# Order of the slots on PE in a macaron layer (MoE, attention, MoE): gate, up and down in one run, attention visits two by two

## The reference, cut to what matters

```
x = x + 0.5 * ffn(layernorm(x))
x = x + attention(layernorm(x))
x = x + 0.5 * ffn(layernorm(x))
```

```
g, u = split(x @ w_gu.T)
acc += (silu(g) * u) @ w_d.T * combine[:, expert]
```

## Time and profile before

| what | value |
|---|---|
| median of 3 runs | 2342.43 us (2339.06 to 2343.24) |
| profiled execution, its own time | 2340.71 us |
| its span, first to last instruction | 2338.9 us |
| mean granted TensorE clock over the span | 0.998 |
| PE busy | 2241.6 us, 96% |
| DVE busy | 1580.5 us, 68% |
| ACT busy | 1236.9 us, 53% |
| POOL busy | 1051.4 us, 45% |
| matmuls L1071 (gate, up) | 9216 |
| matmuls L1089 (down) | 4608 |
| matmuls L1134 (values) | 2048 |
| matmuls L1101 and L1113 (scores) | 1024 each |

### The profile page before, as it was taken

One profiled execution on the slowest core, in us unless ns is written; L12 is line 12 of the kernel. 1 busy time (PEld: TensorE's weight loads), 2 busy tenths in 40 slices (PEclk: granted clock), 3 DMA queues, 4 the chain that ended last, 5 costly groups with the idle time before them and its releaser, 6 DMA issues.

```text
span 2338.9 us, 47968 instructions
## 1 busy us (share of the span) xinstructions
PE 2241.6 (96%) x19280; PEld 1499.3 (64%) x19280; DVE 1580.5 (68%) x3131; ACT 1236.9 (53%) x1966; POOL 1051.4 (45%) x863
## 2 busy tenths in 40 slices
PE   0899999999999999999999999999999999999999
PEld 0788875555565566555555565655655665688887
DVE  7657578877777877777877876776776753355543
ACT  3333331566566666566566566656656666533332
POOL 0667663433443443443434433433433434466665
PEclk9999999999999999999999999999999999999999
DMA  5211121001101011101101111010010010001010
GB/s 198 78 38 33 30 57 37 20 16 40 25 21 42 21 25 32 41 3 40 45 6 45 24 31 32 11 41 11 22 35 16 12 39 10 20 28 30 19 38 19
DMA packets 111446, 77.78 MB, mean 33 GB/s; under 512 B 57460, under 2 KB 103796, under 8 KB 110840
## 3 DMA queue, kind: packets, MB, share of 16 engines
q1 hardware_dynamic: 111080, 74.69, 11.6%
q10 hardware_dynamic: 144, 0.03, 0.0%
HBM read 62.87 MB, written 11.80 MB: 32 GB/s over the span
## 4 chain that ended last, share of the span: by engine, by line
PE 89%; DVE 8%; issue 2%; ACT 0%; DMA 0%; POOL 0%; POOLq 0%; DVEq 0%; ACTq 0%
PE PS L1071 42%; PE PS L1089 21%; PE PS L1101 11%; PE PS L1134 10%; DVE arena L871 1%; PE PS L1113 1%; PE PS L1030 1%; PE PS L1053 1%; PE PS L1175 1%; PE PS L1161 1%; DVE turned L839 1%; DVE turned L837 1%; DVE arena L843 1%; DVE arena L848 1%; DVE arena L836 0%
## 5 line engine op out<-in xcount | busy, mean ns | idle before, releaser
L1071 PE MATMUL PS<-XT,WGU 128*128 128x256 f16 x9216 | 1117.6, 274 | 64.4 <-DVE WGU L725 31.4
L1071 PEld LDWEIGHTS PS<-XT,WGU 128*128 128x128 f16 x9216 | 876.8, 98 | 290.7 <-issue 141.8
L535 POOL TENSOR_TENSOR arena<-arena 128x512 f16<-128x512 f32 x384 | 447.9, 1166 | 1163.6 <-ACT arena L610 1163.6
L871 DVE TENSOR_REDUCE arena<-PS 128x1 f32<-128x512 f32 x1024 | 658.1, 685 | 354.5 <-PE PS L1101 352.7
L633 ACT ACTIVATE arena<-PS,fac 128x512 f32<-128x512 f32 x1024 | 646.4, 684 | 249.2 <-PE PS L1113 247.8
L603 ACT ACTIVATE arena<-PS,fac 128x512 f32<-128x512 f32 x384 | 263.9, 687 | 718.8 <-PE PS L1071 718.8
L1089 PE MATMUL PS<-WD,arena 128*128 128x256 f16 x4608 | 568.0, 273 | 3.2 <-POOL arena L535 1.6
L1089 PEld LDWEIGHTS PS<-WD,arena 128*128 128x128 f16 x4608 | 431.9, 98 | 144.8 <-issue 90.6
L530 POOL TENSOR_TENSOR arena<-arena 128x512 f32<-128x512 f32 x384 | 491.9, 1281 | 47.2 <-DVE arena L856 45.2
L848 DVE SCALAR_TENSOR_TENSOR arena<-arena,PS 128x512 f32<-128x512 f32 x384 | 261.2, 680 | 278.6 <-ACT arena L603 278.1
L1101 PE MATMUL PS<-arena 48*128 48x512 f16 x1024 | 311.7, 381 | 2.7 <-DVE arena L871 2.2
(11 more groups left out here) (112 smaller groups left out, 788.4 us busy)
## 6 DMA issues: line engine op xcount, KB each, us to landing
arena<-ce_scratch SPq DMA_DIRECT2D x256, 128.0 KB, 3.3
arena<-wgu SPq DMA_DIRECT2D x2, 3072.0 KB, 15.0
arena<-q_scratch SPq DMA_DIRECT2D x192, 32.0 KB
arena<-ktab_c SPq DMA_DIRECT2D x16, 256.0 KB, 4.1
q_scratch<-arena SPq DMA_DIRECT2D x32, 128.0 KB, 1.7
out<-X SPq DMA_DIRECT2D x8, 512.0 KB, 2.9
X<-wd SPq DMA_DIRECT2D x1, 3072.0 KB, 25.3
X<-x SPq DMA_DIRECT2D x1, 3072.0 KB, 14.6
```

The lines of the kernel that those rows point to most:

```text
L535: pool.tensor_tensor(hs[1][:, d % HS, :], tw[d % 2], hs[0][:, d % HS, :], ALU.subtract).then_inc(lo_done, 1)
L871: dve.tensor_reduce(mx[:, half * REP * QT + c:half * REP * QT + c + 1], PS[:, B_MAX + half, :], AX_X, ALU.max).then_inc(max_taken, 1)
L1071: ins = pe.matmul(PS[:, b, j * HALF_G:(j + 1) * HALF_G], WGU[w][:, kt, part * CHUNKS + c + j, :], XT[r][:, k % 2, kt, half * HALF_G:(half ...
```

## The change

The table of visits gives positions 2 and 3 in every slot and positions 0 and 1 in addition in every tenth slot (slots d with (d - 64) % 10 == 9); while v is below 0, all four. PE's iteration becomes: gate of d+1, positions 0 and 1 (every tenth slot), up of d+1, down of d-1, positions 2 and 3, one event. An even visit comes first and an odd one second, so a block is scores, values, scores. The event table holds one event for each slot: fixed events keep their slots, and out_T, tok_T and out_y go to the next slot that is free. The loops of ACT and DVE get the same places. By the two tables, visit 0 moves from slot 77 to 74 and the last visit from 310 to 307.

```diff
--- before.py
+++ after.py
@@ -72,6 +72,7 @@
 QKV = 3
 RING = 3
 HEAD_AT = (1, 3, 0, 2)
+EXTRA_EVERY = 10
 FIRST = 2 * PER_GROUP + 16
 
 
@@ -79,7 +80,7 @@
 
     at, v, d = {}, -AHEAD, FIRST
     while v < VISITS + 2:
-        for pos in range(3 if v < 0 or (d - FIRST) % 5 == 4 else 2):
+        for pos in range(0 if v < 0 or (d - FIRST) % EXTRA_EVERY == EXTRA_EVERY - 1 else 2, 4):
             if v < VISITS + 2:
                 at[d, pos] = v
                 v += 1
@@ -128,21 +129,17 @@
                 at[k * PER_GROUP + s].append((name, k + 1, 0))
 
     def place(d, event):
-        while len(at[d]) > 1:
+        while at[d]:
             d += 1
         at[d].append(event)
         return d
 
-    done = 0
-    for hv in range(2 * UNITS):
-        d = place(max(done, SLOT_OF[quad_visit(8 * hv + 7)] + 1), ("out_T", hv, 0))
-        done = d
-        if hv % 4 == 3:
-            d = place(d + 3, ("tok_T", hv // 4, 0))
-            d = place(d + 1, ("tok_T", hv // 4, 1))
-            d += 1
-            for j in range(4):
-                d = place(d + 1, ("out_y", hv // 4, j))
+    turned_at = [place(SLOT_OF[quad_visit(8 * hv + 7)] + 1, ("out_T", hv, 0)) for hv in range(2 * UNITS)]
+    for v in range(2 * UNITS // 4):
+        d = place(turned_at[4 * v + 3] + 3, ("tok_T", v, 0))
+        d = place(d + 1, ("tok_T", v, 1)) + 1
+        for j in range(4):
+            d = place(d + 1, ("out_y", v, j))
     return at
 
 
@@ -669,8 +666,9 @@
                 k, s = divmod(d, PER_GROUP)
                 if d + 1 < SLOTS:
                     gate(d + 1)
-                if (d, 0) in VISIT:
-                    visit(VISIT[d, 0])
+                for pos in range(2):
+                    if (d, pos) in VISIT:
+                        visit(VISIT[d, pos])
                 if 0 <= d < SLOTS:
                     high(d)
                 if 1 <= k <= GROUPS:
@@ -683,12 +681,9 @@
                         rows_high(norm_of_group(k + 1))
                     if s == T_LOGITS + 1:
                         exponentials(k + 1)
-                if (d, 1) in VISIT:
-                    visit(VISIT[d, 1])
-                if len(EVENTS[d]) > 1:
-                    event(d, 1)
-                if (d, 2) in VISIT:
-                    visit(VISIT[d, 2])
+                for pos in range(2, 4):
+                    if (d, pos) in VISIT:
+                        visit(VISIT[d, pos])
                 if EVENTS[d]:
                     event(d, 0)
 
```

## The result

The changed kernel takes 2472.94 us (median of 4 runs, 2467.82 to 2475.31), the kernel before 2342.49 in the same comparison: ratio 1.0563, 95% interval 1.055 to 1.0576. It is 130 us slower, where 111 was forecast, and lies inside the stated range of 2400 to 2505.

A forecast was written before the change was run, and what follows sets the result against it. PE, with 89% of the chain that ended last, was taken as the bound, with what it waits for. Terms of -23 + 18 + 25 + 21 + 33 + 13 + 7 + 14 + 5 = +113 us gave 2453 us, range 2400 to 2505.

The forecast's parts named there:

- changes of tiling: On PE, a block of two visits has four changes instead of five: 255 blocks at 0.09 us, -23 us.
- waits inside blocks: Second scores wait for the first visit's second maximum and exponential: 0.07 us in 256 blocks, +18 us (3 to 41).
- joins: Up waits behind join events, pieces at 1.82, 2.88 and 2.75 us: 42.6 less 17.1, +25 us.
- row transposes and tok_T: Up waits for ACT's copy behind these events: 0.5 us each in 43 events, +21 us.
- out_T: Up waits for DVE's normalising: 12 with DVE free, 0.3 us each; 17 behind a piece, 1.7 each; +33 us.
- out_y, with logits: Up behind out_y: 9 with a piece ahead on DVE, 1.4 us each; plain ones and logits nothing; +13 us.
- max_rows ahead of events: In 7 slots a unit's `max_rows` falls in front of an event, about 1 us each: +7 us.
- visits below 0: Slots 64 to 73, four visits each, wait for DVE's maxima: 87 us for ten slots, +14 us.
- clock: Five drops of the clock after PE's waits of 2 to 3 us: +5 us, bounds 0 and 40.
- The backlog: DVE and ACT are 1.18 and 1.24 us behind PE when it leaves a score block; events directly behind meet this.
- Rival (A): Long waits between gate and up each drop the clock: 35 drops, ten blocks at half speed, 2518 us; chance 0.12.

The follow-up runs named there:

- E7: Kernel before, plus one full-width matmul between values and scores of 235 odd visits: 2388.62 us, ratio 1.0206.
- E8: Kernel before, plus the same 235 full-width matmuls placed ahead of the values, adding no change of tiling: 2367.69 us, ratio 1.0112.
- E2: Changed kernel, with the event directly behind down and ahead of the block of positions 2 and 3 in all engines: 2454.99 us, ratio 1.0493.
- E4: Changed kernel, with visits below 0 three to a slot (positions 0, 2 and 3) instead of four: 2452.39 us, ratio 1.0483.
- E3: Changed kernel, plus twelve full-width matmuls ahead of up behind a join, unless the additional block follows: 2457.66 us, ratio 1.0507.
- E1: Changed kernel, with the event's step ahead of the norm and router pieces on DVE: 2429.59 us, ratio 1.0383.
- E5: Changed kernel, regular block between gate and up, additional one behind down, three visits a slot below 0, ACT's tanh between the exponentials: 2389.21 us, ratio 1.0215.

## Why the prediction was right

**The sum.** Forecast +113 on the profiled execution, measured 2474.11 - 2340.71 = +133. The timeline of the changed kernel, read from start to start, gives this beside the forecast's terms:

| term | forecast | measured |
|---|---|---|
| changes of tiling, 255 x 0.09 | -23 | -23 (0.089 each, E7 less E8) |
| waits inside blocks | +18 | +24, and second scores late +10 |
| joins | 42.6 - 17.1 | 43.6 - 18.3 |
| row transposes and tok_T | +21 | +20 |
| out_T | +33 | +25 |
| out_y, with logits | +13 | +16 |
| max_rows ahead of events | +7 | inside the terms above |
| visits below 0 | +14 | 23 - 7 = +16 |
| clock | +5 | +27 |

The other waits of the kernel before, 15 us, are gone from or taken up by these rows, and some 7 us of waits at down and at scores are new; the measured column then comes to about +133 within a few us.

**The backlog.** The step that carried the forecast was that DVE and ACT are 1.18 and 1.24 us behind PE when it leaves a block, and that an event directly behind it must wait for both. Transposes behind scores took 2.15 us until ACT's copy ended, said, and each lost 0.45 where 0.5 was forecast. E2 shows that it is this meeting and not the missing cover: with 2.2 us more cover only 18 us came back.

**The joins.** In all 43.6 us against 42.6, and that these sums agree to 1 us is luck. The prices were too favourable for the second piece (2.88 forecast, 3.33 measured, once 3.75) and the third (2.75, and 3.33); the first is right (1.82, and 1.89 in four of five, once 2.31). The 15 pieces without the additional block, which make up the 43.6, come to 37.4 by the forecast's prices (5 x 1.82 + 6 x 2.88 + 4 x 2.75). The three with it were put at some 2 us each, 5.2 together, and held up by only 0.3 each: their wait went into the block, whose second scores wait for DVE, and that is counted among the late second scores. The delay by the statistics was sized well (DVE began at 2.44, supposed 2.5). What was missing is the join's last step, which took 1.19 to 1.28 us instead of 0.69 in nine of the twelve second and third pieces, 0.5 to 0.6 more each (last section).

**out_T and out_y.** A plain out_T lost 0.06, not 0.3: in the one at 607.29, DVE's first step began 1.01 behind the transposes, not 1.18, and gate 0.50 behind them, not 0.44. The 16 behind a piece or `max_rows` lost 0.55 to 3.56 us, 1.45 on average, where 17 x 1.7 was said. So out_T was put 8 us too high, which hid part of what the clock took.

**Visits below 0.** 87 us forecast for ten slots, 88 measured (the gate of slot 65 starts at 340.2, that of slot 75 at 428.5). The picture behind the figure was wrong: the prediction had all four in a row, but the code puts two behind gate and two behind down. DVE was the bound in both pictures, which is why the figure held; E4 agrees, for with three visits instead of four PE's idle time fell from 19 to 10.9 us. That the figure held to 1 us with a wrong picture is partly luck.

**The clock.** This is the term that was mis-sized: "five drops: +5 us" stands against 27. Between the start and the end of its span the changed kernel has 15 stretches at the lower level, 58 us together. Each lies at or just behind the end of a wait of PE of 1.5 us or more: 11 at a second or third join, two behind out_T, one behind out_y, one among the visits below 0. So there were three times as many drops as said, and one costs more than the 1 us of the 2 us window that the earlier trace rows showed, about 1.8 (27 / 15), since the clock is still at 0.63 in the next 2 us. E3 ties these drops to idle waits. Rival (A) had the right mechanism and nearly the right price (1.7 us), but 35 drops instead of 15, and it had the clock down through all ten slots of the visits below 0, where one drop came.

The Trainium skill (TensorE: Matmul & The Clock Gate, Why this matters for your kernels) says in general that idle gaps between bursts should be avoided. The rows agree.

**In-block waits and the saving.** 0.07 us was forecast and 0.07 measured in the ordinary block, against 0.09 saved: an ordinary block gains 0.02 us. The Trainium skill (TensorEngine Tiling, Key Properties) has a change of mode drain the engine. Scores to values at 0.54 and E7 less E8 agree with it.

## What to carry to other kernels

Before grouping work on the busy engine, look how far behind the engines are that empty its banks, at the moment it leaves the group: here 1.2 us, which every bank handed over directly afterwards pays, whichever of the two comes first. A fixed cost saved per switch (0.09 us) is to be set against the wait that the closer spacing makes (0.07 us), before anything else is counted. And a wait of PE costs more than its length when the clock falls behind it; where a wait can't be removed, full-width matmuls without a use in it were worth some 15 us in this kernel.

## What the runs showed of the hardware that was not expected

**DVE's last join step was stretched by POOL.** L838 adds two operands that both lie in SBUF. In the changed kernel 9 of the 18 joins inside the attention's slots took 1.19 to 1.28 us for it, the others 0.68 to 0.69. In the case shown, POOL's L532 ran from 1223.75 to 1224.90 and L838 ended 0.54 behind it, at 1225.44; the next third piece is the same, with POOL from 1236.23 to 1237.38 and L838 up to 1237.92. All nine began while L532 was running and ended 0.54 or 0.55 behind its end, and none of the others did. Where L838 began first and L532 during it, five times, L838 kept its 0.69 and L532 took 1.28 to 1.71 instead of 1.15. DVE's L851, one operand of which is in PSUM, began during an L532 305 times in the same profile and took its 0.69 each time. In the kernel before none of these 18 joins met POOL like that (two of the six joins ahead of the attention did, and took 1.23 and 1.24); the new order put the step beside it. In E1, E2 and E5 the joins came at another moment, and all 18 took 0.68 to 0.70. No run moved POOL's step by itself.

The Trainium skill (GPSIMD Engine Reference, Specifications) says that POOL shares its SBUF interfaces with VectorE and contends with DVE instructions that have two SBUF inputs. The trace agrees.

**Work inside waits paid.** 180 full-width matmuls inside waits made the kernel 15.3 us faster (E3), 13 by the ratios, and the mean granted clock rose from 0.987 to 0.993, which is worth as much.

**The price of a change of tiling** is the same in the starts of single matmuls (0.09) and, within its noise, in total time (20.9 us for 235, 0.089 each), and between two tiled shapes it is the same as to full width (a score block takes 0.54 until the values or until a full-width matmul).
